# Residual add and output store in 512 KB pieces instead of 256 KB, and the first weight chunks of the second attention fetched one group earlier

## What is computed

```python
xn  = layernorm(x)                                   # no scale or shift
# attention: every 4th token of a 2048-token segment, 16 heads of 64, causal
q, k, v = split(xn[0::4] @ w_in.T + b_in)
att = softmax(causal(q @ k.T / 8)) @ v @ w_out.T + b_out   # zero for the other tokens
# feed-forward: a shared part and 8 experts, the best 6 by router weight
shared = (silu(xn @ ws1) * (xn @ ws2)) @ ws3
probs  = softmax(xn @ wr); w = top6(probs) / sum(top6(probs))
routed = sum_e w[e] * (silu(xn @ w1[e]) * (xn @ w2[e])) @ w3[e]
out = x + att + shared + routed
```

## Time and profile before

| | us |
|---|---|
| median of 2 runs | 976.3 (973.0 to 979.6) |
| the profiled execution | 974.0 |
| its span on the slowest core (core 2) | 972.5 |
| spans of the eight cores | 961.7 to 972.5 |
| PE busy / share | 750.1 / 77% |
| DVE, ACT, POOL busy | 274.2, 280.3, 104.6 |
| mean granted TensorE clock, core 2 | 0.871 |

### The profile page before, as it was taken

The page is one execution under the profiler, slowest core; times in us unless marked ns, Lnnn a source line. Parts: engine busy times, 40 slices in busy tenths (PEclk is TensorE's granted clock), DMA queues, the critical chain, the costliest instruction groups (busy, mean ns, idle before and its releaser), DMA issues.

```text
span 972.5 us, 12462 instructions; the slowest of 8 cores (961.7 to 972.5 us)
## 1 busy us (share of the span) xinstructions
PE 750.1 (77%) x4320; PEld 346.9 (36%) x4320; DVE 274.2 (28%) x580; ACT 280.3 (29%) x472; POOL 104.6 (11%) x149
## 2 busy tenths in 40 slices
PE   1386678428999689689697488888999698899884
PEld 1234434213443234234243134434444233344331
DVE  2414514412300350351151025324220152131220
ACT  1234234301112441451442045333111353211211
POOL 3010214010011002001101100000001100201102
PEclk9997677657999899799898678977999989999998
DMA  5366949951026305403613813120004411703407
GB/s 100 99 75 118 130 45 132 143 74 21 1 33 118 110 1 108 130 23 69 153 39 63 196 27 84 23 44 1 1 1 96 122 44 14 161 1 76 98 3 170
DMA packets 51147, 71.61 MB, mean 74 GB/s; under 512 B 21136, under 2 KB 23184, under 8 KB 51088
## 3 DMA queue, kind: packets, MB, share of 16 engines
q0 software_dynamic: 37264, 37.26, 28.4%
q1 hardware_dynamic: 13824, 33.56, 10.6%
HBM read 74.50 MB, written 16.78 MB: 94 GB/s over the span
## 4 chain that ended last, share of the span: by engine, by line
PE 54%; DMA 18%; ACT 10%; DVE 8%; issue 7%; POOL 1%; DVEq 0%; ACTq 0%; SPq 0%; POOLq 0%
PE pA L829 8%; PE pB L829 7%; PE pQ L894 7%; PE pK L894 6%; DMA osb<-x 6%; DMA WinNat<-w_out 5%; PE pA L464 4%; PE pA L773 4%; DMA WinNat<-w_in 4%; PE pA L482 3%; PE pB L773 3%; DMA out<-osb 3%; DVE st_s L350 2%; DVE HP L851 2%; DMA XF<-x 2%
## 5 line engine op out<-in xcount | busy, mean ns | idle before, releaser
L829 PE MATMUL pA<-XN,W 128*128 128x512 bf16 x512 | 129.8, 412 | 47.7 <-ACT s1e L847 32.4
L914 POOL DMA_DIRECT2D osb<-x x64 | 54.4, 863 | 582.3 <-ACT osb L909 578.8
L829 PE MATMUL pB<-XN,W 128*128 128x512 bf16 x512 | 115.7, 379 | 0.0
L829 PEld LDWEIGHTS pA<-XN,W 128*128 128x128 bf16 x512 | 51.2, 104 | 117.9 <-issue 72.9
L829 PEld LDWEIGHTS pB<-XN,W 128*128 128x128 bf16 x512 | 50.1, 98 | 60.5
L851 DVE TENSOR_TENSOR HP<-s1e,pB 128x1024 bf16<-128x1024 bf16 x32 | 39.1, 1221 | 110.4 <-PE pB L829 79.3
L796 DVE TENSOR_TENSOR HS<-HS,pB 128x512 bf16<-128x512 bf16 x16 | 10.5, 685 | 197.0 <-ACT HS L787 186.1
L894 PE MATMUL pQ<-W,HP 128*128 128x512 bf16 x256 | 63.3, 392 | 0.0
L847 ACT ACTIVATE s1e<-pA 128x1024 bf16<-128x1024 f32 x32 | 32.7, 1023 | 103.0 <-PE pA L829 102.9
L894 PE MATMUL pK<-W,HP 128*128 128x512 bf16 x256 | 60.7, 380 | 0.0
L210 PE MATMUL ptT<-ident,WinNat 128*128 128x128 bf16 x128 | 16.2, 306 | 55.4 <-DMA WinNat<-w_out 27.7
(11 more groups left out here) (138 smaller groups left out, 960.4 us busy)
## 6 DMA issues: line engine op xcount, KB each, us to landing
XF<-x SPq DMA_DIRECT2D x32, 512.0 KB, 4.6
osb<-x POOLq DMA_DIRECT2D x64, 256.0 KB, 4.9
out<-osb SPq DMA_DIRECT2D x64, 256.0 KB, 4.0
WinNat<-w_in POOLq DMA_DIRECT2D x40, 256.0 KB, 4.7
W<-w POOLq DMA_DIRECT2D x16, 256.0 KB, 11.4
W<-w POOLq DMA_DIRECT2D x1, 2048.0 KB, 36.2
WinNat<-w_out POOLq DMA_DIRECT2D x8, 256.0 KB, 4.0
Ws<-ws POOLq DMA_DIRECT2D x3, 512.0 KB, 11.9
```

Source lines behind the costliest of these rows:

```text
L829: ins = t.matmul(bview[bn], Wx[:, e, ci, :], XN[:, rb, ci, :], start=(ci == 0), stop=(ci == CI - 1))
L914: em("gpsimd", lambda g, seg=seg, r=r, q=q, Hh=Hh, dst=dst: g.dma_start(out=dst, in_=xv[seg, r, q][:, 512 * Hh:512 * (Hh + 1)], accum_op=A ...
```

## The change

Two edits, and a third that goes with the first.

1. `out_sb` becomes two pieces of 1024 columns. The two halves of a tile are still two matmul chains and two ACT copies, but one DMA adds `x` to both (512 KB) once both copies are done, and one DMA stores both (512 KB). There are 32 of each in place of 64. Only the first half's copy waits for the store that used the piece before.
2. The tail calls `ln_pump` twice for each tile instead of once.
3. `stream_qk(0, 0)` for segment 1 is emitted before `ffn_group(0, 3)` instead of before `attention(1)`.

```diff
-        out_sb = A(nc.sbuf_tensor("osb", [P, 4, 512], F32))
+        out_sb = A(nc.sbuf_tensor("osb", [P, 2, 1024], F32))
...
                 for q in range(NQ):
+                    sl2 = state["fin_slot"] % 2
+                    state["fin_slot"] += 1
+                    evs = []
                     for Hh in range(2):
...
-                        sl4 = state["fin_slot"] % 4
-                        state["fin_slot"] += 1
-                        dst = out_sb[:, sl4, :]
-                        ew = [("sp", cf), ("sst%d" % sl4, 16 * state["st_uses"][sl4])]
-                        ce = em("scalar", lambda s, dst=dst, bn=bn: s.activation(
-                            out=dst, in_=bview[bn], func=AF.Identity),
-                            waits=ew, inc="sa")
+                        ew = [("sp", cf)]
+                        if Hh == 0:
+                            ew.append(("sst%d" % sl2, 16 * state["st_uses"][sl2]))
+                        ce = em("scalar", lambda s, Hh=Hh, bn=bn, sl2=sl2: s.activation(
+                            out=out_sb[:, sl2, 512 * Hh:512 * (Hh + 1)], in_=bview[bn],
+                            func=AF.Identity), waits=ew, inc="sa")
                         bank[bn] = ("sa", ce)
-                        state["acc_uses"][sl4] += 1
-                        em("gpsimd", lambda g, seg=seg, r=r, q=q, Hh=Hh, dst=dst: g.dma_start(
-                            out=dst,
-                            in_=xv[seg, r, q][:, 512 * Hh:512 * (Hh + 1)],
-                            accum_op=ALU.add),
-                            waits=[("sa", ce)], inc="sacc%d" % sl4, k=16)
-                        em("sync", lambda sy, seg=seg, r=r, q=q, Hh=Hh, dst=dst: sy.dma_start(
-                            out=ov[seg, r, q][:, 512 * Hh:512 * (Hh + 1)],
-                            in_=dst),
-                            waits=[("sacc%d" % sl4, 16 * state["acc_uses"][sl4])],
-                            inc="sst%d" % sl4, k=16)
-                        state["st_uses"][sl4] += 1
+                        evs.append(ce)
+                    state["acc_uses"][sl2] += 1
+                    em("gpsimd", lambda g, seg=seg, r=r, q=q, sl2=sl2: g.dma_start(
+                        out=out_sb[:, sl2, :], in_=xv[seg, r, q], accum_op=ALU.add),
+                        waits=[("sa", evs[0]), ("sa", evs[1])], inc="sacc%d" % sl2, k=16)
+                    em("sync", lambda sy, seg=seg, r=r, q=q, sl2=sl2: sy.dma_start(
+                        out=ov[seg, r, q], in_=out_sb[:, sl2, :]),
+                        waits=[("sacc%d" % sl2, 16 * state["acc_uses"][sl2])],
+                        inc="sst%d" % sl2, k=16)
+                    state["st_uses"][sl2] += 1
+                    ln_pump()
                     ln_pump()
...
+                if seg == 0 and r == NR - 1:
+                    stream_qk(0, 0)
                 ensure_group(seg, r)
                 ffn_group(seg, r)
                 if seg == 0 and r == NR - 1:
                     flush_tail()
                     ensure_group(1, 0)
-                    stream_qk(0, 0)
                     attention(1)
```

More of the change, by code:

```diff
@@ L957, in build_nc @@
         em("sync", lambda sy: sy.nop(),
-           waits=[("sst%d" % i, 16 * state["st_uses"][i]) for i in range(4)])
+           waits=[("sst%d" % i, 16 * state["st_uses"][i]) for i in range(2)])
         ninstr = {e: len(sch[e]) for e in ENGS}
```

## The result

| | us |
|---|---|
| changed kernel, median | 995.0 |
| kernel before, median of the runs beside it | 976.9 |
| ratio, 95% interval | 1.018 (1.015 to 1.022) |
| profiled execution of the changed kernel, its span | 986.5, 985.0 (core 5) |

The change costs 18 us by the medians, 1.8%. The profiled execution is the quickest of the changed kernel's, so the rows of its slowest core explain only 12.5 us of span (972.5 to 985.0); where the other executions lost more isn't recorded.

A forecast was written before the change was run, and what follows sets the result against it. Bound: in tails of ten matmuls, a piece's way through copy, add and store, not PE; at `attention(1)`, waiting for chunks. Terms 2.4 + 13.2 + 1.5 + 12.0 + 7.1 - 10.3 = +25.9 on 974.0: 1000 us, range 976 to 1010.

The forecast's parts named there:

- e5: Fifth copy to `out_sb` in a tail of ten matmuls: forecast 15.8 us after the first copy, 10.8 before.
- e8: Eighth, last copy to `out_sb` in a tail of ten matmuls: forecast 23.1 us after the first, +6.0 against 17.1.
- halfway: Rival: each 512 KB add lands only 1.0 us later than one of 256 KB; 985 us in all, chance 0.14.
- The wait for the piece: Tails of ten matmuls: the fifth copy waits for the first pair's add and store, PE idling 5 to 6 us.
- The price of an add: Cost goes with bytes: a 512 KB add takes 58 engine-us and lands in 6.2 us, +2.0 against 256 KB.
- The first rival: DMA cost goes per packet, not per byte, so the larger DMAs gain: 940 us, chance 0.12.
- The clock: Tails of ten matmuls: after some 6 us idle PE's clock falls, making the seventh half 2.0 us slower.
- e7: Seventh copy to `out_sb` in a tail of ten matmuls: forecast 20.8 us after the first copy.
- Tails with XF behind them: Tails (0, 1) and (0, 2): the next `XF` load stands behind the last store; +6.6 us each, 13.2 together.
- The 1.5 us for the two chunks beside `XF`: Behind tail (0, 1) the two early chunks share the DMA engines with the `XF` load: 0 to 3.6 us, taken as 1.5.
- Attention: Start of `attention(1)`: the Q product no longer waits for chunks, 8.6 us earlier and 1.7 faster at full pace, -10.3.
- Tails with 19 matmuls: Tails (0, 0) and (1, 0): copies don't wait, dearer last add and store cost +1.2 us each, 2.4 together.

The follow-up runs named there:

- big3: The changed kernel with three pieces of 1024 columns in `out_sb` instead of two: 959.0 us, ratio 0.986 to the kernel before.
- adds256: The changed kernel with each add halved to 256 KB, issued when its own half is copied; stores stay 512 KB: 978.9 us, ratio 1.004.
- pieces_only: The kernel before with the pieces of 1024 columns and the doubled `ln_pump`, without the move of `stream_qk`: 1003.6 us, ratio 1.030.
- hoist_only: The kernel before with only the move of `stream_qk(0, 0)` to before `ffn_group(0, 3)`, four pieces of 512 columns: 961.5 us, ratio 0.987.

## Why the prediction was right, step by step

The mechanism came as forecast, and the sum of it was too large: +25.9 against +18. The likeliest outcome on record, slower by over 2% (0.56), isn't settled: the ratio is 1.018 and its interval (1.015 to 1.022) holds 2%. The growth of the add, the time of e5 and that of e8 lie between the forecast (+2.0, 15.8, 23.1) and the rival "halfway" (+1.0, 14.2, 21.6): +1.3, 14.4 to 15.4 and 21.5 to 23.1.

**The wait for the piece: right.** "12.8 + 3.0 = 15.8 for e5 (bounds 12.8 and 16.8)": 14.4 to 15.4. "PE idle 5 to 6 us there": 5.06 in tail (0, 1), 4.87 in tail (0, 3). big3 shows that this wait is the loss.

**The price of an add: right in kind, too high in size.** I said 58 engine-us and 6.2 us to land; it was 50 and 5.5. The store was to land in 3.2 and landed in 2.6. Together that puts e5 0.4 to 1.4 early, and the load of `XF` and the end by as much. The first rival, cost per packet, is out: 29 became 50. By the line of the Trainium skill for DMAs of the gpsimd path (DMA: Bandwidth & Descriptors, "Anatomy of one DMA — SWDGE (gpsimd) path") 256 KB more would add an estimated 0.6 us to the landing. The add, which goes that way, gained 1.3, so the line doesn't fit it. Merging didn't pay here, and the add's growth isn't the whole reason: the merged add also starts later.

**The clock: the fall was right, its balance was not.** This is the term with the wrong size in tails (1, 1) and (1, 2): 2.0 us were added to every tail of ten matmuls for a slow seventh half. It came (4.2 us from its first matmul to e7), but part was given back just behind. Windows of the changed kernel's tail (0, 1), the seventh half and the first expert matmuls (length, busy times, granted clock, DMA share, GB/s):

```profile
387.00:392.00 5.00, 3.99 (x11) 1.50 (x12) 0.00 (x0) 1.09 (x2) 0.84 (x1) 0.66 0.54 134
396.50:400.50 4.00, 3.58 (x17) 1.69 (x18) 2.21 (x4) 0.77 (x2) 0.86 (x2) 1.00 0.89 160
```

The seventh half ran at 0.66, as forecast. But the expert matmuls behind the tail ran at full clock, 1.00, where before they had a granted 0.70 (391.0 to 396.1). The same place behind tail (1, 2), changed kernel:

```profile
915.36 3.61 PE L829 MATMUL pA<-XN,W 128*128 128x512 bf16 x16 [2.43 <-ACT HS L787]
```

and kernel before:

```profile
906.22 5.21 PE L829 MATMUL pA<-XN,W 128*128 128x512 bf16 x16 [3.06 <-ACT HS L787]
```

PE idled 2.43 us there with the change and 3.06 before; in tail (0, 1), 1.88 and 2.90. The eighth copy, for which it waits, no longer waits for a store of its own: it follows the eighth half at PE's pace. 16 matmuls take 3.61 us instead of 5.21 (granted clock 1.00 and 0.69). It is no chance of one core: behind tails (1, 1) and (1, 2) they run at full pace on all eight cores with the change, and on two of eight before. So 1.6 of the 2.0 us come back wherever the expert matmuls are what the group goes on with, which is in (1, 1) and (1, 2). There the price was 6.0; less 1.6 for this and 0.9 for an e8 at 22.2 instead of 23.1 it is 3.5. Measured: +3.6 and +3.2 (+3.1 and +4.0 by the medians over the cores).

Why the clock stays up there is open. The shorter idle alone doesn't decide it. At the same place in adds256 PE idled 2.43 us on all eight cores, and then ran the 16 matmuls at full pace on three and slowly on five. Cores 1 and 2 of it (granted clock 1.00 and 0.67):

```profile
894.33 3.61 PE L829 MATMUL pA<-XN,W 128*128 128x512 bf16 x16 [2.43 <-ACT HS L787]
...
893.87 5.30 PE L829 MATMUL pA<-XN,W 128*128 128x512 bf16 x16 [2.43 <-ACT HS L787]
```

On the three fast cores the seventh half had been slow (e7 5.3 us after e5), as in most tails of the changed kernel; on the five slow ones e7 had come 3.5 to 4.9 after e5. That is no rule either, for behind tail (1, 2) of the changed kernel three cores have full pace with 4.7 to 4.8. I ran nothing on it by itself.

**Tails with XF behind them: right, 6.6 forecast, +5.4 and +4.8.** Here the path goes by the last store and the load, so the clock gives nothing back; the difference is the price of the DMAs. The 1.5 us for the two chunks beside `XF` don't show on the slowest core, where the load behind tail (0, 1) takes 5.00 us in the chain and that behind (0, 2) 4.93. They do show on the others. The layer norm that waits for the load starts 34.8 to 39.2 us after the first copy on the eight cores, median 36.7, where pieces_only, without the early chunks, has 33.8 to 36.2, median 34.5; behind tail (0, 2) the two have medians of 35.2 and 35.0. The term was right, and that it seems absent is an accident of the core.

**Attention: right in kind, and the close number is luck.** -10.3 forecast, -10.6 on the slowest cores, but -8.5 by the medians over the cores. hoist_only shows the part without the longer tail: 17.1 on the slowest cores and 14.8 by the medians, where I had 17.6. I had priced it from the core on which the Q product came latest, 31.7 us after the first copy, where the median of the eight is 29.9.

**Tails with 19 matmuls: nothing, +1.2 forecast twice.** By the medians +0.1 and +0.3. The add and store prices again.

**The sum.** +25.9 forecast, +12.5 in the profiled execution and +18 by the medians, which fell between. Of the 13.4 us too much, 5.2 lie in the two stretches where the clock was given back, 4.5 in the two with `XF` and chunks behind them, 2.2 at the end and 2.0 in the long tails. This is by the rows of two cores, which are good to a few us a stretch. Apart from the clock's 3.2 I put them down mainly to the price of the DMAs, which was too high in every term; that is a reading of the table, not an experiment.

## What to carry to other kernels

A buffer between a compute engine and a chain of DMAs is priced by when a piece of it comes free: merging two transfers delays the first byte, keeps twice the bytes until the last one is out, and halves the number of pieces, all in one edit. If transfers are to be merged, give the buffer more pieces (here a third was enough). And look at what else stands in the queue that the merged chain goes through: here the loads for the next tiles stood behind the stores, and moving them (one rule about where a load is put in) was worth more than any size of a piece (31 us, 949.9 to 918.9). And when two profiles are compared stretch by stretch, look at all eight cores: the slowest core of one profile can be the worst at just the place that is priced.

## What the runs showed of the hardware

An accumulating DMA of 128 rows took 29 engine-us at 2 KB a row and 50 at 4 KB; a plain store 11.7 and 21. An add thus took 2.4 to 2.5 times the engine time of a store of the same bytes. The granted clock could fall behind an idle of PE of under 2 us: in hoist_only, behind tail (0, 0) on the slowest core, PE idled 1.93 us and the next 16 matmuls had a granted 0.70 and took 5.08 us instead of 3.61. But the length of the last idle doesn't settle it: 2.43 us at one place of adds256 was followed by 1.00 on one core and 0.67 on another.
